# Attention on one core: seven single PSUM banks in a ring, exponentials by half units, maxima cut in two parts on GpSimd

## The chip, the core and the metric

The kernel runs on one core of a Trainium2 chip. The metric is device time in microseconds; three runs of the kernel before had a median of 1662.29 us (1660.99 to 1663.57). TensorE is called PE, VectorE DVE, ScalarE ACT, GpSimd POOL and SyncE SP, as in the profile.

## The reference

A two-layer block over 8 sequences of 512 tokens with 256 features: cross attention with 16 heads of 16 dimensions, a mixture of experts, a second cross attention, and a linear layer with simulated fp8. Only the two attentions matter here:

```python
qh = _split_heads(q @ q_map, R); kh = _split_heads(k @ k_map, R); vh = _split_heads(k @ v_map, R)
scores = jnp.einsum('brqd,brkd->brqk', qh, kh) * scale
weights = jax.nn.softmax(scores, axis=-1)
out = jnp.einsum('brqk,brkd->brqd', weights, vh)
```

## The kernel before

`attention(S, l)` runs twice, for l = 0 and l = 1. A *group* is one sequence and four heads; there are 32 groups (NG), n = 0 to 31, and each has 8 *units* (U), numbered i. The softmax subtracts a maximum for each query, and both the maximum and the exponential need a product of q and k, so the product is made twice:

- `max_unit` (L340) makes the products of two heads for 128 queries, two matmuls of 512 columns in a pair of PSUM banks. DVE's `take_maxima` (L346) reduces the pair to 2 numbers per query. The maxima run AHEAD = 14 units in front of the scores, so that of PE's 256 score units the first 242 (PAIRED) are each followed by a maximum unit.
- When the 8 maxima units of a group are reduced, `turn_maxima` on DVE cuts the maxima into a rounded part (a cast, L1137) and a remainder (a subtraction, L1139), and transposes both (L1143). SP moves them with four DMAs (`move_maxima`, L361) into rows of q of the group to come, where the score product subtracts them. PE's first score unit of that group waits for it (`mrow`).
- `score_unit` (L1062) makes the scores less maxima, two matmuls into another pair of banks; ACT takes the exponential of the whole pair (L1120, 128x1024) into SBUF.
- `values` (L1074) multiplies exponentials by values: for each unit half of a 128-key tile of an earlier unit, four matmuls (eight in the trace, two passes each), accumulating in `pout`. After a group's last one ACT copies `pout` to SBUF (L1111) and SP stores it (L996) and loads it back in another layout.
- POOL issues the ten DMAs that load q and k of the group four ahead (`load`, L415), once the scores of a group are all made and its buffers are free, and in layer 0 adds a bias to X once in four groups (L1043).

Each engine runs its own queue in the written order, with semaphores between them. PE's order for a unit is score, maximum, values. The eight PSUM banks are three pairs (`ring`) and two single banks (`pout`), and pairs go round over the uses maximum, score, maximum, score. So score unit s waits until maxima unit s-1 (counted from the 14 ahead) is reduced, and the maximum unit behind it waits until the exponential of score unit s-1 is taken:

```python
if s: e.wait_ge(reduced, s)
score_unit(n, i)
if s + 1 < PAIRED:
    if s: e.wait_ge(exped, s)
    max_unit(AHEAD + s + 1)
```

Of the kernel before, what the change touches and what calls it, by code (L numbers as in the profile page):

```python
# [14 lines left out]
P = 128  # L15
# [269 lines left out]
BLOCK = 32  # L285

# [49 lines left out]
def max_products(e, bank, q, k, i):  # L336
    t, p = i // 2, i % 2
    for hh in range(2):
        at = slice(HALF * hh, HALF * (hh + 1))
        mm = e.matmul(bank[:, hh, :], q[at, p, t * P:(t + 1) * P], k[at, p, :], start=True, stop=True)  # L340
    return mm


def take_maxima(e, nmax, bank, i):
    t, p = i // 2, i % 2
    return e.tensor_reduce(nmax[:, :].rearrange("p (x y t) -> p x y t", x=2, y=2)[:, :, p, t], bank[:, :, :],  # L346
                           AX.X, ALU.max, negate=True)

# [15 lines left out]
class Ahead:  # L364
# [7 lines left out]
    def make(self, e, m):  # L372
# [5 lines left out]
        max_products(e, self.banks[m % 2], self.inputs.q[n], self.inputs.k[n], m % UNITS).then_inc(self.made, 1)  # L378
# [555 lines left out]
def attention(S, l):  # L934
# [6 lines left out]
    with ctx:  # L941
# [8 lines left out]
        ring = [ps(f"ring{j}", [P, 2, SEQ]) for j in range(3)]  # L950
        pout = [ps(f"pout{j}", [P, SEQ]) for j in range(2)]
# [14 lines left out]
        def max_bank(m):  # L966
            return ring[(AHEAD + 2 * (m - AHEAD)) % 3]

        def score_bank(s):
            return ring[(AHEAD + 1 + 2 * s if s < PAIRED else AHEAD + PAIRED + s) % 3]  # L970

        def spread_bank(b, kd):
            return score_bank(NG * U - 3 + b)[:, kd, :]
# [10 lines left out]
        with nc.Block() as block:  # L984
# [40 lines left out]
            def _(e):  # L1025
# [3 lines left out]

                for j in range(EARLY_GROUPS, G):  # L1030
# [18 lines left out]
            def _(e):  # L1049
                def max_unit(m):  # L1050
# [3 lines left out]
                    max_products(e, max_bank(m), q[n % G], k[n % G], i).then_inc(maxed, 1)  # L1054

                def score_unit(n, i):
# [3 lines left out]
                    for hh in range(2):  # L1060
                        at = slice(HALF * hh, HALF * (hh + 1))
                        mm = e.matmul(score_bank(n * U + i)[:, hh, :], k[j][at, p, t * P:(t + 1) * P], q[j][at, p, :],  # L1062
# [3 lines left out]
                def values(n, t, half):  # L1066
                    b, g = n // G, n % G
                    if t == 0 and half == 0:
                        if n >= 2:
                            e.wait_ge(taken, n - 1)  # L1070
                    e.wait_ge(exped, n * U + 2 * t + 2)
                    at = slice(half * D, (half + 1) * D)
                    for h in range(HG):
                        mm = e.matmul(pout[n % 2][32 * h:32 * h + VW, at], v[:, b * TPB + t, g * HG + h, :], pexp[t][:, h, at],  # L1074
# [3 lines left out]
                e.wait_ge(clear, 2)  # L1078
                max_unit(AHEAD)
                for n in range(NG):  # L1080
                    for i in range(U):
                        s = n * U + i
                        if s < PAIRED:
                            if s:
                                e.wait_ge(reduced, s)
                        elif s == PAIRED + 1:
# [1321 lines left out]
```

## Time and profile before

| | |
|---|---|
| median of three runs | 1662.29 us |
| span of the profiled execution | 1670.2 us |
| attention l = 0 in the span, about | 120 to 457 us |
| attention l = 1 in the span, about | 1227 to 1563 us |
| DVE reduces of maxima in the two stages | 484, mean 1220 ns |
| ACT exponentials | 512, mean 1026 ns |
| ACT copies of outputs | 64, about 0.59 us |

The profiled execution is one execution, taken by the hardware profiler; its span runs from the first to the last instruction. Start times count from the span's start. In the timeline view a row holds like instructions of one engine merged, with start, duration and count, and in brackets the idle time before and what ended it. A score unit is a row L1062 on PE with x2, a maximum unit a row L340 with x2, values a row L1074 with x8. PEld is the load of the weights. Starts of the same engine's instructions are closer than their durations, since they are pipelined.

### The profile page before, as it was taken

The page shows a single profiled execution, that of the slowest core. Times are in us where ns is not written, and L with a number is a line of the kernel's source. Part 1 is how long each engine was busy: PE and PEld are TensorE (multiplying, and loading weights), DVE is VectorE, ACT ScalarE, POOL GpSimd, SP SyncE. Part 2 cuts the span into 40 slices and gives each one's busy share as a digit, 9 for nine tenths or more (in the row PEclk, how much of TensorE's full clock was granted, in tenths as well). Part 3 has the DMA queues.
Part 4 walks back from the last instruction along what each step waited for, and adds up shares of the span by engine and source line. Part 5 has one row for each costly group of instructions (what it writes and reads, how often), then busy time and mean ns, then how long its engine had stood idle before and what let it go on. Part 6 is the DMA issues. An engine that isn't in the chain of part 4 may idle for free. (4 is left out here: it accounts for less than half of the span.)

```text
span 1670.2 us, 28397 instructions
## 1 busy us (share of the span) xinstructions
PE 1513.5 (91%) x10910; PEld 979.2 (59%) x10910; DVE 1293.5 (77%) x2074; ACT 977.5 (59%) x1238; POOL 637.3 (38%) x957
## 2 busy tenths in 40 slices
PE   7989999999996289999999999779979999999846
PEld 6863333333385279999999999745523333333434
DVE  6789999999665856657665564379889999999787
ACT  5547888888833134444444444336548888888544
POOL 4314555555122135344342332255324444443120
PEclk9989999999996589999999999979979999999986
DMA  8974565555263022222223221168745555554103
GB/s 277 326 204 94 122 122 123 122 123 123 68 259 101 27 64 87 82 77 78 84 82 93 70 79 36 44 213 286 219 93 123 123 123 122 123 123 103 34 0 101
DMA packets 118742, 198.58 MB, mean 119 GB/s; under 512 B 29568, under 2 KB 63680, under 8 KB 117584
## 3 DMA queue, kind: packets, MB, share of 16 engines
q1 hardware_dynamic: 83840, 111.22, 21.9%
q0 software_dynamic: 33360, 83.94, 20.1%
q8 instruction: 87, 1.43, 0.4%
q10 hardware_dynamic: 1408, 1.61, 0.3%
q14 instruction: 47, 0.39, 0.1%
HBM read 117.77 MB, written 77.87 MB: 117 GB/s over the span
## 5 line engine op out<-in xcount | busy, mean ns | idle before, releaser
L1120 ACT ACTIVATE i_room<-a_ring 128x1024 f32<-128x1024 f32 x512 | 522.5, 1026 | 130.8 <-PE a_ring L1062 130.7
L346 DVE TENSOR_REDUCE logit<-a_ring 128x2 f32<-128x1024 f32 x484 | 576.9, 1220 | 26.7 <-PE a_ring L340 26.4
L1074 PE MATMUL a_pout<-i_room,values 128*17 128x256 f32 x4096 | 321.7, 387 | 0.7 <-ACT i_room L1120 0.7
L1755 ACT ACTIVATE e_full<-e_pH,b1T 128x320 f32<-128x320 f32 x256 | 135.0, 527 | 247.0 <-PE e_pH L1696 236.3
L1704 PE MATMUL e_pY<-fc_w,e_hid_hi 128*128 128x512 f32 x640 | 237.1, 407 | 0.6 <-DVE e_hid_lo L1808 0.6
L1062 PE MATMUL a_ring<-i_qk 64*128 64x512 f32 x768 | 194.9, 504 | 2.6 <-DVE logit L346 1.9
L1705 PE MATMUL e_pY<-fc_w,e_hid_lo 128*128 128x256 f32 x640 | 179.8, 281 | 0.0
L1062 PEld LDWEIGHTS a_ring<-i_qk 64*128 64x128 f32 x768 | 72.8, 186 | 169.7 <-DVE logit L346 103.1
L340 PE MATMUL a_ring<-i_qk 64*128 64x512 f32 x712 | 165.5, 461 | 6.0 <-DVE a_pout L1169 5.2
L1816 POOL DMA_INDIRECT w<-normed,slot_get x80 | 84.4, 1055 | 225.7 <-PE fc_turned L1681 199.6
L1808 DVE TENSOR_TENSOR e_hid_lo<-e_full,e_hid_hi 128x640 fp32r<-128x640 f32 x128 | 119.5, 934 | 55.7 <-ACT e_hid_hi L1764 55.7
L1696 PE MATMUL e_pH<-e_rowsT_hi,fc_w1T_hi 128*128 128x320 f32 x512 | 159.5, 312 | 0.0
L1696 PE MATMUL e_pH<-e_rowsT_lo,fc_w1T_hi 128*128 128x320 f32 x512 | 159.0, 311 | 0.0
L1696 PE MATMUL e_pH<-e_rowsT_hi,fc_w1T_lo 128*128 128x320 f32 x512 | 158.4, 309 | 0.0
L1074 PEld LDWEIGHTS a_pout<-i_room,values 128*17 128x17 f32 x4096 | 68.3, 95 | 129.7 <-issue 126.7
L1704 PEld LDWEIGHTS e_pY<-fc_w,e_hid_hi 128*128 128x128 f32 x640 | 120.3, 188 | 24.3 <-DVE e_hid_lo L1808 0.9
L1705 PEld LDWEIGHTS e_pY<-fc_w,e_hid_lo 128*128 128x128 f32 x640 | 121.3, 189 | 0.0
L1833 POOL DMA_INDIRECT ytok<-e_y,slot_put x80 | 82.7, 1034 | 93.0 <-DVE e_y L1788 78.3
L415 POOL DMA_DIRECT2D i_qk<-key_centre x42 | 24.1, 573 | 212.2 <-PE a_ring L1062 212.2
L1764 ACT ACTIVATE e_hid_hi<-e_full 128x640 fp32r<-128x640 f32 x128 | 94.6, 739 | 11.8 <-ACT e_full L1755 0.4
L1696 PEld LDWEIGHTS e_pH<-e_rowsT_hi,fc_w1T_hi 128*128 128x128 f32 x512 | 96.7, 189 | 5.6
L340 PEld LDWEIGHTS a_ring<-i_qk 64*128 64x128 f32 x712 | 67.9, 187 | 53.2 <-ACT i_room L1120 30.6
(334 smaller groups left out, 2530.2 us busy)
## 6 DMA issues: line engine op xcount, KB each, us to landing
ks<-i_room SPq DMA_DIRECT2D x64, 256.0 KB, 4.1
outs<-a_osb SPq DMA_DIRECT2D x64, 256.0 KB, 2.8
qs<-i_room SPq DMA_DIRECT2D x60, 256.0 KB, 4.7
fc_raw<-in_L_ffn_fc_w SPq DMA_DIRECT2D x15, 1024.0 KB, 5.4
i_qk<-ks POOLq DMA_DIRECT2D x84, 128.0 KB, 3.5
i_qk<-qs POOLq DMA_DIRECT2D x84, 128.0 KB, 3.6
BIG<-outs SPq DMA_DIRECT2D x64, 128.0 KB
ytok<-r_zeros SPq DMA_DIRECT2D x8, 1024.0 KB, 9.6
```

Of the source, the lines that this page charges most:

```text
L340: mm = e.matmul(bank[:, hh, :], q[at, p, t * P:(t + 1) * P], k[at, p, :], start=True, stop=True)
L346: return e.tensor_reduce(nmax[:, :].rearrange("p (x y t) -> p x y t", x=2, y=2)[:, :, p, t], bank[:, :, :], AX.X, ALU.max, negate=True)
L1062: mm = e.matmul(score_bank(n * U + i)[:, hh, :], k[j][at, p, t * P:(t + 1) * P], q[j][at, p, :], start=True, stop=True)
L1074: mm = e.matmul(pout[n % 2][32 * h:32 * h + VW, at], v[:, b * TPB + t, g * HG + h, :], pexp[t][:, h, at], start=(t == 0 and half == 0), st ...
L1120: e.activation(pexp[t][:, 2 * p:2 * p + 2, :], score_bank(n * U + i)[:, :, :], ACT.Exp).then_inc(exped, 1)
L1696: mm = e.matmul(pH[h][:, 0:WIDE], w1T[x][pl][:, k, f * P:(f + 1) * P], rowsT[j][pr][:, k, h * WIDE:(h + 1) * WIDE], start=(k == 0 and n_pa ...
L1704: e.matmul(pY[t][:, :, :], hid[s % 3][HI][:, token], w2[x][:, f, :, :], start=(f == 0), stop=False)
L1705: mm = e.matmul(pY[t][:, HI, :], hid[s % 3][LO][:, token], w2[x][:, f, HI, :], start=False, stop=(f == KF - 1))
L1755: e.activation(full[s % 2][:, h * WIDE:(h + 1) * WIDE], pH[h][:, 0:WIDE], ACT.Silu, bias=S.b1T[:, n * KF + f:n * KF + f + 1]).then_inc(act, 1)
L1764: e.activation(hid[s % 3][HI][:, :], full[s % 2][:, :], ACT.Copy).then_inc(hi, 1)
L1808: e.tensor_tensor(hid[s % 3][LO][:, :], full[s % 2][:, :], hid[s % 3][HI][:, :], ALU.subtract).then_inc(lo, 1)
L1816: e.indirect_dma_start(rows[:, t, :], None, S.normed[:, :], bass.IndirectOffsetOnAxis(ap=S.slot_get[:, c:c + 1], axis=0)).then_inc(ldr[0 i ...
```

## The change

- **PSUM.** The ring is one tensor of seven single banks, `pout` has one bank. A use takes two neighbouring banks modulo 7. Since 7 is odd, one maxima unit in seven falls on the last and the first bank; DVE reduces it in two instructions (`take_maxima_apart`).
- **ACT.** The exponential of a unit is two instructions of 128x512, each with its own signal. A maximum unit waits only for the first half of the unit before. Score units wait for the exponentials of two units before, too.
- **Values.** With one `pout`, the values that hang over from the group before are made in units 0 (one) and 1 (two) of a group, none in unit 2; ACT copies `pout` after unit 1 and not after unit 3.
- **Maxima.** POOL makes the two parts (`cut_maxima`). In its queue they stand behind the ten load DMAs. DVE transposes two units later than before.

```diff
+BANKS = 7
+VALUE_LAG = 3
+TURN_LAG = 2
+LATE_VALUES = (UNITS - 3,), (UNITS - 2, UNITS - 1)
...
+def take_maxima_apart(e, nmax, banks, i):
+    t, p = i // 2, i % 2
+    for hh in range(2):
+        last = e.tensor_reduce(nmax[:, :].rearrange("p (x y t) -> p x y t", x=2, y=2)[:, hh, p, t:t + 1], banks[hh],
+                               AX.X, ALU.max, negate=True)
+    return last
...
-        ring = [ps(f"ring{j}", [P, 2, SEQ]) for j in range(3)]
-        pout = [ps(f"pout{j}", [P, SEQ]) for j in range(2)]
+        ring = ps("ring", [P, BANKS, SEQ])
+        pout = ps("pout", [P, SEQ])
...
+                def cut_maxima(n):
+                    halves, whole = max_halves(nparts[n % 2]), max_whole(nmax[n % 2])
+                    if n >= 3:
+                        e.wait_ge(nturned, n - 2)
+                    e.wait_ge(reduced, (n + 1) * U - AHEAD)
+                    e.tensor_copy(halves[:, :, 0, :], whole).then_inc(cut, 1)
+                    e.wait_ge(cut, 2 * n - 1)
+                    e.tensor_tensor(halves[:, :, 1, :], whole, halves[:, :, 0, :], ALU.subtract).then_inc(cut, 1)
...
                 for n in range(NG):
-                    if n + G < NG:
-                        load(n + G)
+                    if 0 < n <= NG - G:
+                        load(n - 1 + G)
+                    if n + 1 < NG:
+                        cut_maxima(n + 1)
...
-                        if n >= 2:
-                            e.wait_ge(taken, n - 1)
-                    e.wait_ge(exped, n * U + 2 * t + 2)
+                    if t == 0 and half == 0 and n:
+                        e.wait_ge(taken, n)
+                    e.wait_ge(exped, 2 * (n * U + 2 * t + 2))
...
                         if s < PAIRED:
                             if s:
                                 e.wait_ge(reduced, s)
+                            if s >= 2:
+                                e.wait_ge(exped, 2 * s - 2)
...
                         if s + 1 < PAIRED:
                             if s:
-                                e.wait_ge(exped, s)
+                                e.wait_ge(exped, 2 * s - 1)
                             max_unit(AHEAD + s + 1)
-                        if i >= 3:
-                            values(n, (i - 3) // 2, (i - 3) % 2)
-                        elif n:
-                            values(n - 1, (i + U - 3) // 2, (i + U - 3) % 2)
+                        if i >= VALUE_LAG:
+                            values(n, (i - VALUE_LAG) // 2, (i - VALUE_LAG) % 2)
+                        elif n and i < VALUE_LAG - 1:
+                            for v_unit in LATE_VALUES[i]:
+                                values(n - 1, v_unit // 2, v_unit % 2)
...
-                        e.activation(pexp[t][:, 2 * p:2 * p + 2, :], score_bank(n * U + i)[:, :, :], ACT.Exp).then_inc(exped, 1)
-                        if i == 3 and n:
+                        for hh in range(2):
+                            e.activation(pexp[t][:, 2 * p + hh, :], score_bank(n * U + i, hh), ACT.Exp).then_inc(exped, 1)
+                        if i == 1 and n:
                             take_outputs(n - 1)
...
                 for m in range(AHEAD, NG * U):
                     reduce(m)
-                    if m % U == U - 1:
-                        turn_maxima(m // U)
+                    if m % U == TURN_LAG - 1 and m >= 2 * U:
+                        turn_maxima(m // U - 1)
+                turn_maxima(NG - 1)
```

On DVE, at the start of attention l = 0, before: eight reduces, then the cast, the subtraction and the transposition of a group's maxima.

```order
L346 TENSOR_REDUCE logit<-a_ring 128x2 x8
L1137 CAST logit<-logit 128x2x8
L1139 TENSOR_TENSOR logit<-logit 128x2x8
L1143 STREAM_TRANSPOSE logit<-logit 128x32
L346 TENSOR_REDUCE logit<-a_ring 128x2 x8
```

The same place now; L357 is a maxima unit reduced in two halves.

```order
L350 TENSOR_REDUCE logit<-a_ring 128x2 x6
L1175 STREAM_TRANSPOSE logit<-logit 128x32
L357 TENSOR_REDUCE logit<-a_ring 128x1 x2
L350 TENSOR_REDUCE logit<-a_ring 128x2 x6
L357 TENSOR_REDUCE logit<-a_ring 128x1 x2
L1175 STREAM_TRANSPOSE logit<-logit 128x32
```

The cast and the subtraction are gone from DVE, and 34 of its 242 reduces of an attention have become two.

On POOL, before, a group's work is ten load DMAs and nothing else (in layer 0 sometimes the bias):

```order
L415 DMA i_qk<-key_centre 8x2x512
L415 DMA i_qk<-query_centre 8x2x512
L415 DMA i_qk<-ks 32x2x512
L415 DMA i_qk<-qs 32x2x512
L415 DMA i_qk<-ks 16x2x512
```

Now, the end of one group's loads and the start of the next's:

```order
L427 DMA i_qk<-ks 16x2x512
L427 DMA i_qk<-qs 16x2x512
L1051 CAST logit<-logit 128x2x8 [waits a0_reduced,a0_nturned]
L1053 TENSOR_TENSOR logit<-logit 128x2x8 [waits a0_cut]
L427 DMA i_qk<-key_centre 8x2x512 [waits a0_scored]
L427 DMA i_qk<-query_centre 8x2x512
```

The two parts of the maxima stand behind all ten DMAs of a load that is released two units before the maxima are complete.

On PE, in the second unit of a group, now (before, each unit has one values part, L1074 x4, and the score unit waits only for `reduced`):

```order
L1089 MATMUL a_ring<-i_qk 128x512 [waits a0_exped,a0_reduced]
L1089 MATMUL a_ring<-i_qk 128x512
L344 MATMUL a_ring<-i_qk 128x512 [waits a0_ld0,a0_exped]
L344 MATMUL a_ring<-i_qk 128x512
L1100 MATMUL a_pout<-i_room,values 17x256 [waits a0_exped]
L1100 MATMUL a_pout<-i_room,values 17x256 x3
L1100 MATMUL a_pout<-i_room,values 17x256 [waits a0_exped]
L1100 MATMUL a_pout<-i_room,values 17x256 x3
L1089 MATMUL a_ring<-i_qk 128x512 [waits a0_exped,a0_reduced]
```

One values part has moved from the third unit into the second.

## Rows read from the trace of the kernel before

**Rows 1.** Busy time by engine in one stretch (us), granted clock, DMA share, GB/s

```profile
300.00:400.00 100.00, 99.86 (x918) 38.40 (x920) 95.03 (x107) 81.27 (x86) 55.90 (x100) 1.00 0.50 121
```

**Rows 2.** Timeline of all engines, 300 to 312 us: PE and ACT

```profile
301.89 0.50 PE L1062 MATMUL a_ring<-i_qk 64*128 64x512 f32 x2
302.22 0.41 PE L340 MATMUL a_ring<-i_qk 64*128 64x512 f32 x2
302.43 1.02 ACT L1120 ACTIVATE i_room<-a_ring 128x1024 f32<-128x1024 f32 x1 [0.35 <-PE a_ring L1062]
302.56 0.63 PE L1074 MATMUL a_pout<-i_room,values 128*17 128x256 f32 x8
303.11 0.51 PE L1062 MATMUL a_ring<-i_qk 64*128 64x512 f32 x2
303.50 0.50 PE L340 MATMUL a_ring<-a_k,a_q 64*128 64x512 f32 x2
304.49 0.50 PE L1062 MATMUL a_ring<-i_qk 64*128 64x512 f32 x2
```

**Rows 3.** Timeline of the same stretch: the turning of the maxima and its release

```profile
303.93 0.18 DVE L1137 CAST logit<-logit 128x16 fp32r<-128x16 f32 x1
304.42 0.21 DVE L1143 STREAM_TRANSPOSE logit<-logit 128x32 f32<-128x32 f32 x1
304.56 1.19 DVE L346 TENSOR_REDUCE logit<-a_ring 128x2 f32<-128x1024 f32 x1
...
305.80 0.19 PEld L1062 LDWEIGHTS a_ring<-i_qk 64*128 64x128 f32 x2 [0.52 <-DVE logit L346]
```

**Rows 4.** Timeline of the same stretch: POOL's ten loads

```profile
300.50 0.51 PE L1062 MATMUL a_ring<-i_qk 64*128 64x512 f32 x2
...
301.31 0.57 POOL L415 DMA_DIRECT2D i_qk<-key_centre  x1 [5.30 <-PE a_ring L1062]
...
306.05 0.50 POOL L415 DMA_DIRECT2D i_qk<-qs  x1
...
311.83 0.57 POOL L415 DMA_DIRECT2D i_qk<-key_centre  x1 [5.28 <-PE a_ring L1062]
```

**Rows 5.** Timeline of ACT in the same stretch: output copy, next exponential

```profile
307.27 0.59 ACT L1111 ACTIVATE a_osb<-a_pout 128x512 f32<-128x512 f32 x1
307.75 1.03 ACT L1120 ACTIVATE i_room<-a_ring 128x1024 f32<-128x1024 f32 x1
```

**Rows 6.** Single lines: durations ns min/median/max, first and last start

```profile
L263 POOL TENSOR_TENSOR r_product<-r_mv,r_rstd x8: 198/198/198, 471.8 to 515.4; 128x4 f32<-128x4 f32 x8
L1043 POOL TENSOR_TENSOR X<-X,bo_b x8: 2380/2390/2398, 148.6 to 422.4; 128x1024 f32<-128x1024 f32 x8
```

**Rows 7.** Timeline outside attention: small POOL operations, alone and beside DVE

```profile
75.49 0.21 POOL L241 TENSOR_SCALAR p_var<-p_mv 128x4 f32<-128x4 f32 x1 [6.29 <-DVE p_mv L236]
...
1184.12 1.19 DVE L447 TENSOR_TENSOR i_room<-c_full_k,i_room 128x1024 fp32r<-128x1024 f32 x1
...
1184.29 1.11 POOL L241 TENSOR_SCALAR c_var<-c_mv 128x4 f32<-128x4 f32 x1 [3.72 <-DVE c_mv L236]
1185.48 1.03 POOL L244 TENSOR_TENSOR c_rstd<-c_var,half 128x4 f32<-128x4 f32 x1
```

**Rows 8.** Timeline, 1097 to 1099 us: a DVE instruction that waits for POOL

```profile
1097.71 1.12 POOL L244 TENSOR_TENSOR c_rstd<-c_var,half 128x4 f32<-128x4 f32 x1
1098.94 0.48 DVE L1945 SCALAR_TENSOR_TENSOR X<-BIG,c_rstd,X 128x256 f32<-128x256 f32 x1 [0.22 <-POOL c_rstd L244]
```

**Rows 9.** Timeline of POOL at the start of attention: first two loads

```profile
133.30 0.68 POOL L415 DMA_DIRECT2D i_qk<-key_centre  x1 [10.55 <-PE a_ring L1062]
...
143.35 0.57 POOL L415 DMA_DIRECT2D i_qk<-key_centre  x1 [4.69 <-PE a_ring L1062]
```

**Rows 10.** SP in the stretch of Rows 2, and the landing of output stores

```profile
304.66 2.63 SPq L361 DMA_DIRECT2D i_qk<-logit  x4
DMA to landing us min/median/max: 2.0/2.8/4.3
```

More of the change, by code:

```diff
@@ L333, in load_half, with max_products @@
             load_group(self.S, self.l, e, n, self.q[n], self.k[n], self.ld[n], range(half * (LOADS // 2), (half + 1) * (LOADS // 2)))
-def max_products(e, bank, q, k, i):
+def max_products(e, banks, q, k, i):
     t, p = i // 2, i % 2
@@ L339, in max_products, with take_maxima @@
         at = slice(HALF * hh, HALF * (hh + 1))
-        mm = e.matmul(bank[:, hh, :], q[at, p, t * P:(t + 1) * P], k[at, p, :], start=True, stop=True)
+        mm = e.matmul(banks[hh], q[at, p, t * P:(t + 1) * P], k[at, p, :], start=True, stop=True)
     return mm
-def take_maxima(e, nmax, bank, i):
+def take_maxima(e, nmax, pair, i):
     t, p = i // 2, i % 2
-    return e.tensor_reduce(nmax[:, :].rearrange("p (x y t) -> p x y t", x=2, y=2)[:, :, p, t], bank[:, :, :],
+    return e.tensor_reduce(nmax[:, :].rearrange("p (x y t) -> p x y t", x=2, y=2)[:, :, p, t], pair[:, :, :],
                            AX.X, ALU.max, negate=True)
+def take_maxima_apart(e, nmax, banks, i):
[4 more added lines that the diff above has]
+    return last
 def max_halves(nparts):
@@ L377, in make @@
             e.wait_ge(self.taken, m - 1)
-        max_products(e, self.banks[m % 2], self.inputs.q[n], self.inputs.k[n], m % UNITS).then_inc(self.made, 1)
+        max_products(e, [self.banks[m % 2][:, hh, :] for hh in range(2)], self.inputs.q[n], self.inputs.k[n], m % UNITS).then_inc(self.made, 1)
     def take(self, e, m):
@@ L964, in attention, with max_first, max_banks, score_bank @@
         oput = [sem(f"oput{j}") for j in range(2)]
[L966 to L970, printed above, removed]
+        def max_first(m):
+            return 4 * (m - AHEAD) % BANKS
+        def max_banks(m):
+            return [ring[:, (max_first(m) + hh) % BANKS, :] for hh in range(2)]
+        def score_bank(s, hh):
+            use = 2 * s + 1 if s < PAIRED else PAIRED + s
+            return ring[:, (2 * use + hh) % BANKS, :]
         def spread_bank(b, kd):
-            return score_bank(NG * U - 3 + b)[:, kd, :]
+            return ring[:, b * KD + kd, :]
         def moved(n):
@@ L1053, in max_unit @@
                         loaded(e, n)
-                    max_products(e, max_bank(m), q[n % G], k[n % G], i).then_inc(maxed, 1)
+                    max_products(e, max_banks(m), q[n % G], k[n % G], i).then_inc(maxed, 1)
                 def score_unit(n, i):
@@ L1110, in take_outputs @@
                         e.wait_ge(oput[n % 2], 16 * (n // 2))
-                    e.activation(osb[n % 2][:, :], pout[n % 2][:, :], ACT.Copy).then_inc(taken, 1)
+                    e.activation(osb[n % 2][:, :], pout[:, :], ACT.Copy).then_inc(taken, 1)
                 inputs.wait_stored(e)
@@ L1131, in reduce @@
                     e.wait_ge(maxed, m + 1 - AHEAD)
-                    take_maxima(e, nmax[n % 2], max_bank(m), m % U).then_inc(reduced, 1)
-                def turn_maxima(n):
-                    halves, whole = max_halves(nparts[n % 2]), max_whole(nmax[n % 2])
-                    e.wait_ge(reduced, (n + 1) * U - AHEAD)
-                    e.tensor_copy(halves[:, :, 0, :], whole).then_inc(cut, 1)
-                    e.wait_ge(cut, 2 * n - 1)
-                    e.tensor_tensor(halves[:, :, 1, :], whole, halves[:, :, 0, :], ALU.subtract).then_inc(cut, 1)
+                    first = max_first(m)
+                    if first + 1 < BANKS:
+                        take_maxima(e, nmax[n % 2], ring[:, first:first + 2, :], m % U).then_inc(reduced, 1)
+                    else:
+                        take_maxima_apart(e, nmax[n % 2], max_banks(m), m % U).then_inc(reduced, 1)
+                def turn_maxima(n):
                     if n >= 3:
```

19 lines of the change are left out of this document (10 added, 9 removed).

## The prediction

> **What bounds the kernel now.** I read the busy times by stretch first, then the timeline of one group of attention, then single lines. In attention PE is busy 99.86 of 100 us at full granted clock, DVE 95, ACT 81 [rows 1]; three engines so close together say that a loop between them may bind rather than one engine. The repeat is exact: POOL's load of one group starts at 301.31 and the next at 311.83, a period of 10.52 us for 8 units, 1.315 us a unit [rows 4].
>
> The timeline shows two kinds of unit. From one score unit to the next PE takes 303.11 - 301.89 = 1.22 us, called 1.23 below, when nothing holds it; the next takes 304.49 - 303.11 = 1.38 [rows 2]. What holds it is the exponential: score at 301.89, exponential from 302.43 for 1.02, and the maximum unit at 303.50 needs that pair of banks; then 0.99 to the score unit at 304.49. This loop over two units costs 2.60 us, 1.30 a unit [rows 2]. DVE adds a little: its turn runs from the cast at 303.93 to the next reduce at 304.56, and the score unit behind it starts at 305.80, released by DVE [rows 3]. So now: PE's own 8 x 1.23 = 9.84 us, and 0.68 of waits, nearly all for ACT and the turn.
>
> **The change, part by part.**
>
> *ACT in halves.* An instruction of 128x512 lasts 0.59, and the next starts 307.75 - 307.27 = 0.48 behind it [rows 5]. The chain above becomes 0.54 + 0.59 + 0.05 + 0.99 = 2.17 us for two units, under PE's 2.46: the wait is gone, alone worth up to about 0.6 us a group. ACT itself needs 17 x 0.48 = 8.2 us a group and is hidden behind PE; were that cover gone it would add nothing until 9.84.
>
> *DVE without cast and subtraction.* From 303.93 to 304.42 DVE is rid of 0.49 us a group [rows 3]. One maxima unit in seven is two reduces of 512 columns. No reduce of 512 columns from PSUM is shown; on ACT two halves last 2 x 0.59 against 1.02 for the whole, 0.16 more [rows 2, 5]. I bound the split by nothing and 0.2, hidden except where DVE has the deciding reduce (some 4 groups of 28, 0.03 a group on average), and take 0.
>
> *Values doubled in unit 1.* A values part takes 303.11 - 302.56 = 0.55 [rows 2]. Unit 1 lasts 1.23 + 0.55, unit 2 is as much shorter. PE's sum is unchanged, but the maxima unit behind the third score comes later, which DVE reaches late in turn. ACT's copy meets that gap.
>
> *The cuts on POOL.* Here the stall goes. Let L be the start of a group's load. The ten DMAs run from 301.31 to 306.05 + 0.50 = 306.55, 5.24 us [rows 4]. The cuts stand behind them, though the maxima are complete at L + 2.6 (303.93 against 301.31) [rows 3, 4]. DVE asks for them two units later: the last score of the group before is at L - 0.81 (300.50 against 301.31) [rows 4], so scores 0 and 1 are at L + 0.42 and L + 1.65, score 2 is 1.78 later at L + 3.43; its maximum product comes 0.33 later and is reducible about 0.45 behind its start (estimate, it lasts 0.41 and DVE must wake), and the reduce needs 1.22, so DVE is at the transposition at L + 5.4. POOL is not ready: cast 0.21, by the small one-input operation at 75.49 [rows 7]; a gap to the dependent one of 0.08, as at 1185.40 to 1185.48 [rows 7]; subtraction 0.22, from 0.198 for 4 columns [rows 6] plus 12 columns at 2.1 ns (2390 ns for 1024); 0.11 until DVE starts, as from 1098.83 to 1098.94 [rows 8]; 0.05 for the gap behind the last DMA and a second wait (estimate). Together 0.67, ready at L + 5.91. DVE stalls 0.5 us in each group, and this becomes a loop of its own:
>
> - transposition to next reduce 0.14, reduce 1.19, score 0.05: 305.80 - 304.42 = 1.38 [rows 3]
> - two more units to the last score of the group, at PE's pace: 2.46 [rows 2]
> - that score to the next load: 0.81 [rows 4]
> - ten DMAs: 5.24 [rows 4]
> - cuts and wakes: 0.67
>
> That is 10.56 us, against 10.52 now. The gains in ACT, PE and DVE all fall inside the stall; the loop doesn't contain them.
>
> May POOL's small operations be much dearer? At 1184.29 L241 took 1.11 us, at 75.49 the same operation took 0.21. The long one overlaps a DVE operation with two SBUF inputs that ends at 1185.31, and it ends just behind it, at 1185.40 [rows 7]. In attention DVE reduces from PSUM, and the bias addition directly behind loads is constant at 2380 to 2398 ns [rows 6]. So I take the low value, with 1.11 as the upper bound.
>
> The Trainium skill (GPSIMD Engine Reference, Key points) says that GpSimd shares its SBUF interfaces with VectorE and contends with instructions in a 2-port mode or with two SBUF inputs; the two rows agree, and by it the low price holds here, since neither reduce nor transposition is of that kind.
>
> The same page (Engine selection) speaks against the change: two-input elementwise work belongs on VectorE, GpSimd being about twice as slow; by that the subtraction would be an estimated 0.35 rather than 0.22, and the total some 7 us more, which the 198 ns row does not bear out.
>
> *The move, two units later.* The four DMAs start 0.24 behind the transposition and take 2.63 to issue, the last starting at about + 2.25 [rows 3, 10]. The first score of the next group is at + 1.38 + 3 x 1.23 = + 5.07. So the last DMA has 2.8 us to land, and DVE's 0.5 of slack takes in 0.4 more. Small DMAs show no landing here; output stores of 256 KB land in 2.0 to 4.3, median 2.8 [rows 10]. A 4 KB one should be near the low end: I cost it at nothing. SP's stores and reloads of outputs, behind it in its queue, come two units later; ACT needs that buffer only a group later.
>
> *Sum.* Each attention has 28 loads, 27 periods. The first was short, 143.35 - 133.30 = 10.05 [rows 9], and becomes 10.56: + 0.5. The other 26 gain 0.04 each: + 1.0. Behind the last load no cut is late: about 13 units with maxima remain, at 1.23 instead of 1.315, - 1.1, with + 0.3 for a doubled values part and + 0.2 for the later start, so - 0.6. The 14 units without maxima stay. Together + 0.9, twice + 1.8 us. The profiled execution spans 1670.2, so I expect a span of about 1672; it is 7.9 us over the median, and the same difference on the median of 1662.3 gives 1664.
>
> **The rivals.**
>
> 1. *The cuts are dearer than priced* (slower). Place: POOL behind the ten DMAs. Each 0.1 us costs 54 x 0.1 = 5.4 us, as nothing absorbs it. For it: small POOL operations of 0.5 to 1.1 exist [rows 7], and none of 16 columns is shown. Against: the 2380 to 2398 ns. A cast of 0.5 gives + 16, 1680; of 1.1, + 48, 1712. It decides from + 0.03 us a group.
> 2. *The moved maxima land late* (slower). Above 3.2 us from issue each 0.1 costs 5.4 us: at 3.8, some + 30, 1694. For it: median 2.8 of the stores, and loads in flight. Against: 4 KB, and 2.0 as the least.
> 3. *POOL is a little quicker* (faster): cuts and wakes in 0.55 instead of 0.67 make the period 10.44 and the total - 6.5 + 1.8, about 1657.5.
> 4. *The cuts come in time* (faster), the change doing what halves and ring allow: then the period is 9.84 plus the 0.3 that the doubled values cost, 10.15, giving 54 x 0.37 = 20 us and the ends' 2: 1640. Against: POOL would have to be done by L + 5.4, and its DMAs alone need 5.24.
> 5. *Nothing changes in the period because PE bounds anyway*: excluded by the 1.22 and 1.38 in turn [rows 2].
>
> **How the numbers follow.** Forecast 0.55, rival 1 0.20, rival 2 0.08, rival 3 0.12, rival 4 0.05. Within 0.2% is 3.3 us, about what a measurement of this kernel can tell from no change. Of the forecast's 0.55 about 0.07 falls above 1665.6 (cuts of 0.70 and more) and 0.01 below; so faster 0.18, same 0.47, slower 0.35. The range reaches from rival 3 to the milder half of rival 1: 1656 to 1681. That leaves out rivals 2 and 4 and the dear half of rival 1, 0.2 together. The forecast's own range is 1659 to 1668.
>
> **What would show it.** Right: load starts on POOL 10.5 to 10.6 apart; the cast starting where the tenth DMA ends; the transposition waiting for POOL about 0.5 us in each group; no wait of the maximum units for ACT; score intervals of 1.23 in units 5 to 7, and about 1.8 and 0.7 around unit 2. Wrong: loads 10.15 apart with no wait on POOL (rival 4); a cast of 0.5 or more (rival 1); first score units waiting for the maxima's DMA (rival 2).

## The result

The changed kernel takes 1673.08 us (1671.99 to 1674.41, four runs) against 1662.57 for the kernel before on the same chip (1660.99 to 1663.57): a ratio of 1.0069, 95% interval 1.0054 to 1.0083. It is slower by 0.7%, 10.5 us. The forecast was 1664, the likeliest outcome "within 0.2%"; the time lies in the range of 1656 to 1681, on the slower side. One execution each of two kernels below (3413.7 and 1717.46 us), far above the others of its kernel, is left out of the numbers given.

The profiled execution of the kernel before was 7.9 us above its median, and the excess lies outside attention (the rest of its span is 1002.4 us, in the other thirteen profiles 991.3 to 999.3), so I compare the two attention stages. From the first score unit to the last they took 333.9 and 333.9 us before, 337.5 and 338.8 now: + 8.4 us. The other 2 us of the 10.5 between the medians are not placed by these two profiles. From the first load of a group to the 28th, 27 periods, it was 283.8 and 283.9, and is 289.5 and 290.9.

Busy time by engine of the kernel after, in the stretch of [rows 1], and in three short stretches that are spoken of below:

```profile
core 0: us, PE busy (x) PEld busy (x) DVE busy (x) ACT busy (x) POOL busy (x), PEclk, DMA share, GB/s
300.00:400.00 100.00, 91.87 (x894) 34.01 (x888) 88.51 (x94) 83.67 (x158) 60.29 (x116) 0.98 0.58 120
370.00:372.00 2.00, 1.13 (x4) 0.50 (x4) 1.94 (x2) 0.30 (x1) 0.00 (x0) 0.68 0.03 4
372.00:374.00 2.00, 2.00 (x14) 0.65 (x12) 1.23 (x1) 0.95 (x3) 0.00 (x0) 0.50 0.25 88
374.00:376.00 2.00, 2.00 (x24) 0.64 (x22) 1.74 (x2) 1.68 (x4) 0.49 (x1) 0.97 0.33 99
```

In the first 100 us PE is busy 91.87 us where it was 99.86, DVE 88.51 where it was 95.03. No engine is full any more: the loop that binds has idle time in every one of them.

The timeline of one group, kernel after; POOL, then DVE and SP, then PE. These rows answer to [rows 2 to 4]:

```profile
319.95 0.57 POOL L427 DMA_DIRECT2D i_qk<-key_centre  x1 [4.97 <-PE a_ring L1089]
...
324.69 0.50 POOL L427 DMA_DIRECT2D i_qk<-qs  x1
325.19 0.21 POOL L1051 CAST logit<-logit 128x16 fp32r<-128x16 f32 x1
325.48 0.21 POOL L1053 TENSOR_TENSOR logit<-logit 128x16 fp32r<-128x16 f32 x1
330.41 0.57 POOL L427 DMA_DIRECT2D a_k<-key_centre  x1 [4.71 <-PE a_ring L1089]
...
324.02 1.23 DVE L350 TENSOR_REDUCE logit<-a_ring 128x2 f32<-128x1024 f32 x1 [0.35 <-PE a_ring L344]
325.80 0.21 DVE L1175 STREAM_TRANSPOSE logit<-logit 128x32 f32<-128x32 f32 x1 [0.56 <-POOL logit L1053]
325.94 3.44 DVE L350 TENSOR_REDUCE logit<-a_ring 128x2 f32<-128x1024 f32 x3
329.30 1.28 DVE L357 TENSOR_REDUCE logit<-a_ring 128x1 f32<-128x512 f32 x2
...
326.04 2.64 SPq L373 DMA_DIRECT2D i_qk<-logit  x4
...
324.52 0.50 PE L344 MATMUL a_ring<-i_qk 64*128 64x512 f32 x2 [0.30 <-ACT i_room L1153]
325.51 0.50 PE L1089 MATMUL a_ring<-a_q,a_k 64*128 64x512 f32 x2
327.17 0.50 PE L1089 MATMUL a_ring<-a_q,a_k 64*128 64x512 f32 x2 [0.38 <-DVE logit L350]
328.39 0.50 PE L1089 MATMUL a_ring<-a_q,a_k 64*128 64x512 f32 x2
329.61 0.50 PE L1089 MATMUL a_ring<-a_q,a_k 64*128 64x512 f32 x2
```

Read as the loop of the prediction, with L = 319.95: ten DMAs to 325.19 (L + 5.24), the cast directly behind them, the transposition at 325.80 (L + 5.85) after DVE has waited 0.56 us for POOL, a score unit 1.37 later at 327.17, two more in 2.44, and the next load 0.80 behind that, at 330.41. The period is 10.46 us. The page's list of waits has it in sum, beside the second row that matters, first score units that wait for the moved maxima:

```profile
DVE logit L1175 <- POOL logit L1053: 34.0, 50, 2.3
PE a_ring L1089 <- DMA i_qk<-logit: 4.7, 7, 1.2
```

Most of the 54 periods measure 10.45 to 10.60. Nine do not: 12.98, 13.63, 13.63 and 13.71, always the 13th and the 23rd of an attention; 10.71 right behind the first of them; and 10.97, 10.71, 11.23 and 11.31. POOL's timeline in the first of the long ones, then what DVE and PE do behind it:

```profile
257.81 0.53 POOL L427 DMA_DIRECT2D i_qk<-qs  x1
260.11 0.50 POOL L427 DMA_DIRECT2D i_qk<-ks  x1 [1.77 <-issue]
260.61 0.50 POOL L427 DMA_DIRECT2D i_qk<-qs  x1
261.11 0.21 POOL L1051 CAST logit<-logit 128x16 fp32r<-128x16 f32 x1
...
261.72 0.21 DVE L1175 STREAM_TRANSPOSE logit<-logit 128x32 f32<-128x32 f32 x1 [2.33 <-POOL logit L1053]
...
263.10 0.51 PE L1089 MATMUL a_ring<-i_qk 64*128 64x512 f32 x2 [2.16 <-DVE logit L350]
265.98 0.79 PE L1089 MATMUL a_ring<-i_qk 64*128 64x512 f32 x2
```

POOL stands still for 1.77 us between the eighth and the ninth DMA of a load, for nothing that the profile shows. PE then idles 2.16 us, and soon behind it the two matmuls of the score unit at 265.98 last 0.79 instead of 0.50 us. The stretches above show the second such place: behind the pause the granted clock is 0.68 from 370 to 372 and 0.50 (1.2 of 2.4 GHz) from 372 to 374, and is back at 0.97 from 374 to 376. It falls to 0.50 behind each of the four pauses (0.50 or 0.51 in 265:268, 371:374, 1371:1374 and 1480:1483).

The pause is no work of the change. The kernel before has it too, in the same two loads of each attention:

```profile
262.92 0.53 POOL L415 DMA_DIRECT2D i_qk<-qs  x1
265.22 0.51 POOL L415 DMA_DIRECT2D i_qk<-ks  x1 [1.76 <-issue]
265.72 0.50 POOL L415 DMA_DIRECT2D i_qk<-qs  x1
269.73 0.57 POOL L415 DMA_DIRECT2D i_qk<-key_centre  x1 [3.51 <-PE a_ring L1062]
```

There POOL waits for PE 3.51 us behind it, so it cost nothing.

### The profile page after: what moved, and what is told of

Read it like the earlier page. It is cut to its first block and busy times, and to the rows that moved or that the text cites. A ratio compares the mean times of both kernels' runs of the same rounds, so it can differ in the third digit from the quotient of the medians.

```text
span 1672.0 us, 29457 instructions
## 1 busy us (share of the span) xinstructions
PE 1470.5 (88%) x10910; PEld 954.5 (57%) x10910; DVE 1265.5 (76%) x2016; ACT 1008.9 (60%) x1750; POOL 662.8 (40%) x1081
## 3 DMA queue, kind: packets, MB, share of 16 engines
q8 instruction: 88, 1.44, 0.4%
## 5 line engine op out<-in xcount | busy, mean ns | idle before, releaser
L1153 ACT ACTIVATE i_room<-a_ring 128x512 f32<-128x512 f32 x1024 | 547.3, 609 | 99.3 <-PE a_ring L1089 62.0
L350 DVE TENSOR_REDUCE logit<-a_ring 128x2 f32<-128x1024 f32 x416 | 491.3, 1218 | 32.7 <-PE a_ring L344 29.8
L1100 PE MATMUL a_pout<-i_room,values 128*17 128x256 f32 x4096 | 311.6, 388 | 3.3 <-ACT i_room L1153 1.8
L1089 PE MATMUL a_ring<-i_qk 64*128 64x512 f32 x768 | 190.7, 494 | 23.7 <-DVE logit L350 15.5
L1089 PEld LDWEIGHTS a_ring<-i_qk 64*128 64x128 f32 x768 | 73.2, 187 | 180.3 <-DVE logit L350 127.7
L1100 PEld LDWEIGHTS a_pout<-i_room,values 128*17 128x17 f32 x4096 | 74.8, 96 | 172.8 <-ACT i_room L1153 115.0
L344 PE MATMUL a_ring<-i_qk 64*128 64x512 f32 x712 | 149.6, 416 | 16.8 <-ACT i_room L1153 12.7
L1728 PEld LDWEIGHTS e_pH<-e_rowsT_lo,fc_w1T_hi 128*128 128x128 f32 x512 | 96.9, 189 | 0.0
```

Of the source, the lines that this page charges most:

```text
L344: mm = e.matmul(banks[hh], q[at, p, t * P:(t + 1) * P], k[at, p, :], start=True, stop=True)
L1089: mm = e.matmul(score_bank(n * U + i, hh), k[j][at, p, t * P:(t + 1) * P], q[j][at, p, :], start=True, stop=True)
L1100: mm = e.matmul(pout[32 * h:32 * h + VW, at], v[:, b * TPB + t, g * HG + h, :], pexp[t][:, h, at], start=(t == 0 and half == 0), stop=(t = ...
L1153: e.activation(pexp[t][:, 2 * p + hh, :], score_bank(n * U + i, hh), ACT.Exp).then_inc(exped, 1)
L1728: mm = e.matmul(pH[h][:, 0:WIDE], w1T[x][pl][:, k, f * P:(f + 1) * P], rowsT[j][pr][:, k, h * WIDE:(h + 1) * WIDE], start=(k == 0 and n_pa ...
```

## The experiments

All times are medians, and the ratios are against the kernel before on the same chip (1663.12 us for the first four kernels, 1663.51 for the next four, 1660.61 for the last four). "Period" is the distance of load starts in steady groups.

### The cuts back on DVE, still two units late

```diff
 # GpSimd: cut_maxima and its calls are gone; VectorE:
                 def turn_maxima(n):
+                    e.wait_ge(reduced, (n + 1) * U - AHEAD)
+                    e.tensor_copy(halves[:, :, 0, :], whole).then_inc(cut, 1)
+                    e.wait_ge(cut, 2 * n - 1)
+                    e.tensor_tensor(halves[:, :, 1, :], whole, halves[:, :, 0, :], ALU.subtract).then_inc(cut, 1)
```

> The changed kernel with cast and subtraction back on DVE, directly ahead of the transposition, which stays two units late. Theory A (GpSimd's queue sets the period: load, cuts, transposition, three reduces, last score, next load, 5.85 + 1.37 + 2.44 + 0.80 = 10.46 us, plus some 15 us in all of pauses inside the loads that now reach the path): DVE arrives at L + 5.3 and cuts for 0.5, so the transposition starts at about L + 5.8 again, the period stays near 10.4, but pauses of GpSimd no longer reach the path: 1655 us. Theory B (the loss sits in the ring of seven, the halved exponentials or the doubled values, and GpSimd is only where the wait shows): about 1670 to 1673.

Measured: 1683.0 us, ratio 1.0112 (1.0090 to 1.0133), against about 1655 expected. Both theories missed. Layer 1 did what was expected: period 10.30, 283.2 us for the 27 periods. Layer 0 took 301.9, with periods of 12.6 to 14.8 in six of the seven places within them where POOL adds the bias, which only layer 0 has. DVE and POOL at such a place:

```profile
178.43 1.23 DVE L350 TENSOR_REDUCE logit<-a_ring 128x2 f32<-128x1024 f32 x1 [0.36 <-PE a_ring L344]
179.57 2.46 DVE L1163 CAST logit<-logit 128x16 fp32r<-128x16 f32 x1
182.06 0.17 DVE L1165 TENSOR_TENSOR logit<-logit 128x16 fp32r<-128x16 f32 x1
...
179.62 2.37 POOL L1059 TENSOR_TENSOR X<-X,bo_b 128x1024 f32<-128x1024 f32 x1
```

A cast whose median is 165 ns lasts 2.46 us, until POOL's addition of two SBUF tensors is over. The same holds at seven of the eight additions, with casts of 1.99 to 2.99 us. The two periods of 12.60 ran at full clock (1.00 in 316:322 and 360:366); the four of 14.0 to 14.8 have a granted clock of 0.50 behind the wait (137:143, 185:188, 229:232 and 404:409), so part of the loss is the clock's. Both theories took the cuts on DVE as cheap; beside this addition they are not. A later kernel tests that by itself.

### The cuts amid the load

The same work on the same engines; POOL cuts between its fifth and sixth DMA. `load(n, part)` issues the first or the second five.

```diff
                 for n in range(NG):
                     if 0 < n <= NG - G:
-                        load(n - 1 + G)
+                        load(n - 1 + G, 0)
                     if n + 1 < NG:
                         cut_maxima(n + 1)
+                    if 0 < n <= NG - G:
+                        load(n - 1 + G, 1)
```

> The changed kernel with the cuts on GpSimd between the fifth and the sixth load DMA. Theory A: the cuts are done by about L + 3.3, long before DVE asks at L + 5.3, so neither the wait nor the pauses (which come behind the eighth DMA) reach the path; what is left is PE's own sequence of score intervals without the long one, 10.0 to 10.1 us a group: 1673 - 15 - 54 x 0.4 = 1636 us. Theory B: 1670 to 1673. If the later half load comes too late, first maximum units wait for it and the period is above 10.3.

Measured: 1639.0 us, ratio 0.9854 (0.9837 to 0.9870), period 10.01 to 10.02, 273.2 and 272.8 us for the 27 periods. POOL and DVE in one group:

```profile
311.11 0.51 POOL L427 DMA_DIRECT2D i_qk<-ks  x1
311.61 0.21 POOL L1052 CAST logit<-logit 128x16 fp32r<-128x16 f32 x1
311.91 0.22 POOL L1054 TENSOR_TENSOR logit<-logit 128x16 fp32r<-128x16 f32 x1
312.07 0.52 POOL L427 DMA_DIRECT2D i_qk<-qs  x1
...
312.98 1.23 DVE L350 TENSOR_REDUCE logit<-a_ring 128x2 f32<-128x1024 f32 x1 [0.35 <-PE a_ring L344]
314.12 0.20 DVE L1178 STREAM_TRANSPOSE logit<-logit 128x32 f32<-128x32 f32 x1
```

The transposition follows a reduce with no wait. So the place of the cuts in POOL's queue, not the work, costs the changed kernel about 34 us, pauses included. Rival 4 gave 1640 for cuts in time.

### The cast twice

A dose: one more cast on POOL in each group.

```diff
                     e.wait_ge(reduced, (n + 1) * U - AHEAD)
+                    e.tensor_copy(halves[:, :, 0, :], whole).then_inc(twice, 1)
+                    e.wait_ge(twice, n)
                     e.tensor_copy(halves[:, :, 0, :], whole).then_inc(cut, 1)
```

> The changed kernel with GpSimd's cast made twice. Theory A: the loop has no slack, each group grows by the cast and its gap, 0.21 + 0.08 = 0.29 us, over 54 periods: + 16 us, 1689 us, and load starts 10.75 apart. Theory B (other engines set the pace): within 3 us of 1673.

Measured: 1682.3 us, ratio 1.0108 (1.0088 to 1.0128). The period is 10.74, expected 10.75: 0.28 for the dose, nothing absorbed. The total is only 9.3 us above the changed kernel where 16 were expected. The traces say where the rest is: the four long periods are 12.49 each here (10.74 + 1.75, the bare pause) and not 12.98 to 13.71, and the moves cost less (five first scores waited 2.7 us in sum). Over all 54 periods 8.1 us stand above the steady ones, against 15.6 in the changed kernel. PE idled 2.42 us behind a pause here, longer than in the changed kernel, and its clock stayed at 1.00, behind all four. So what a pause costs in clock differs from kernel to kernel, and I can't say from these traces what decides it.

### The kernel before with POOL's cuts alone

The diff is that of the change in `cut_maxima`, its place behind the loads, and the transposition two units later; pairs of banks, whole exponentials and the values stay as before.

> The kernel before with one part of the change alone: cuts on GpSimd behind the loads, transposition two units later; ring of three pairs, whole exponentials and two output banks stay. Theory A: the loop is 1.38 + 2 x 1.315 (PE held by the exponentials) + 0.80 + 5.24 + 0.61 = 10.66 us instead of 10.52, plus the pauses, some 11 us in all, plus 1: about 1681 us, slower than the whole change. Theory B: about 1660 to 1663, as the kernel before.

Measured: 1682.5 us, ratio 1.0113 (1.0097 to 1.0130), period 10.63 (expected 10.66). The half of the change that moves the cuts costs 19 us alone. The row that says so is DVE's wait:

```profile
307.53 0.21 DVE L1149 STREAM_TRANSPOSE logit<-logit 128x32 f32<-128x32 f32 x1 [0.65 <-POOL logit L1037]
```

Its four periods with a pause also separate the pause from the clock. PE idles 1.89 to 1.90 us behind each pause. Two of the periods are 12.40, the bare pause over 10.63, at a clock of 1.00; the other two are 13.72 and 14.37, with a clock of 0.53 in 375:378 and 0.50 in 1379:1385. The first two rows are the start of the work behind a pause that kept the clock and behind one that lost it, the third is the score unit behind the latter:

```profile
266.37 0.50 PE L1073 MATMUL a_ring<-i_qk 64*128 64x512 f32 x2 [1.89 <-DVE logit L346]
374.48 0.50 PE L1073 MATMUL a_ring<-a_q,a_k 64*128 64x512 f32 x2 [1.90 <-DVE logit L346]
376.13 0.79 PE L1073 MATMUL a_ring<-a_q,a_k 64*128 64x512 f32 x2
```

### The cuts on DVE as soon as the maxima are complete

```diff
                 for m in range(AHEAD, NG * U):
                     reduce(m)
-                    if m % U == TURN_LAG - 1 and m >= 2 * U:
-                        turn_maxima(m // U - 1)
-                turn_maxima(NG - 1)
+                    if m % U == U - 1:
+                        turn_maxima(m // U)
```

with the cast and subtraction in `turn_maxima`, as in the first experiment.

> Ring of seven, halved exponentials and late values kept; cast, subtraction and transposition on DVE as soon as the maxima are complete, as in the kernel before. Theory A with the collision seen in the first run of cuts on DVE (DVE's cast lasted 2.5 to 3.0 us where GpSimd's bias addition ran): here the cast comes at about L + 1.7 to 2.6, the addition at L + 5.3, so they don't meet; DVE has room for the 0.6 us in the gap of the doubled values, and the period is PE's 10.0: about 1639 us, as with the cuts amid the load. Theory B (cuts on DVE are what costs, wherever they stand): 1655 or more.

Measured: 1636.6 us, ratio 0.9844 (0.9819 to 0.9869), period 10.09. This is the ring of seven banks, the halves and the values of the change with the maxima handled as before. They are worth 27 us. DVE's turn stands well ahead of where POOL adds the bias.

### The transposition a unit later still

```diff
-TURN_LAG = 2
+TURN_LAG = 3
```

> The changed kernel with the transposition three units late instead of two. Theory A: DVE asks at L + 6.5, GpSimd is ready at L + 5.85, so the wait on GpSimd is gone and half of the pauses with it. Then the move of the maxima decides: the last DMA starts at L + 6.5 + 2.2 = L + 8.7, the first score unit of the next group wants it at about L + 10.4, so it has 1.7 us. If a small DMA lands in under 1.7 us: 10.0 and about 1642 us. If it lands in 2.0 to 2.5 us: 0.3 to 0.8 late each group, a loop of its own at 10.3 to 10.8: 1655 to 1680 us, with the first score unit of a group waiting for the DMA. Theory B: no change, 1673.

Measured: 1661.5 us, ratio 1.0000 (0.9980 to 1.0021, ten runs). With one unit more of slack POOL is in time but for six groups: many periods are 10.01. The 13th and 23rd of each attention, with the pause in them, are 11.01. Between them stand others up to 11.5, and PE's waits name the cause:

```profile
PE a_ring L1089 <- DMA i_qk<-logit: 15.3, 20, 1.4
```

20 first scores wait for the move, against seven in the changed kernel. The first score comes 1.8 to 3.3 us behind the start of the last of the four DMAs in these cases. This is rival 2, nearly alone: late moves take back what POOL's punctuality gives.

### The halves in the old ring

The kernel before, with exponentials of 128x512; each of the two maximum products waits for its half.

```diff
+                    for hh in range(2):
+                        if m > AHEAD + 1:
+                            e.wait_ge(exped, 2 * (m - AHEAD - 2) + 1 + hh)
+                        at = slice(HALF * hh, HALF * (hh + 1))
+                        mm = e.matmul(max_bank(m)[:, hh, :], q[n % G][at, p, t * P:(t + 1) * P], k[n % G][at, p, :], start=True, stop=True)
```

> The kernel before with one part of the change alone: each exponential in two halves, and each of the two maximum matmuls waits for its half; ring of three pairs, cuts on DVE. Theory: the second half ends 0.54 + 0.49 + 0.59 = 1.62 us behind the score against 1.56 for the whole, so the maximum unit waits as long as before and the period stays at 10.5: 1663 us within 3; the halves pay only with the seventh bank. If halves alone free PE: 10.0, 1635.

Measured: 1677.1 us, ratio 1.0093 (1.0067 to 1.0118), where no change was expected. Period 10.71. The maximum unit that was held now starts early and waits in its middle:

```profile
302.13 0.49 PE L1068 MATMUL a_ring<-i_qk 64*128 64x512 f32 x2
302.47 0.62 PE L1059 MATMUL a_ring<-a_k,a_q 64*128 64x512 f32 x2
303.01 0.63 PE L1080 MATMUL a_pout<-i_room,values 128*17 128x256 f32 x8
303.57 0.50 PE L1068 MATMUL a_ring<-i_qk 64*128 64x512 f32 x2
...
301.45 2.31 ACT L1125 ACTIVATE i_room<-a_ring 128x512 f32<-128x512 f32 x4 [0.35 <-PE a_ring L1068]
```

It lasts 0.62 where a free one takes 0.40, and the held unit is 303.57 - 302.13 = 1.44 us (1.38 before). Two halves take 1.08 us where the whole took 1.02, and the second bank of the pair is needed in the same unit. So halves alone are a loss. With the seventh bank, where the two neighbouring banks come free from different units, they are part of the 27 us gained above. No run has the seven banks with whole exponentials, so what each of the two gives there is not separated.

### The bias addition behind the turn

The first experiment, with POOL's addition held until DVE's turn of that group is over.

```diff
                     if l == 0 and n % G == 1:
+                        e.wait_ge(nturned, n + 1)
                         x = S.X[:, tiles(n // G), :]
```

> The first experiment (cuts on DVE, two units late) with one edit: GpSimd's bias addition in layer 0 waits for the transposition. Theory C (DVE's cast and GpSimd's two-input addition exclude each other, in layer 0 alone): the casts last 0.17 again, layer 0 becomes as fast as layer 1 of that run, where 28 loads took 283 us instead of 302: 1683 - 20 = 1663 us. If the stalls stay, something else of that kernel makes them: 1680 or more.

Measured: 1659.9 us, ratio 0.9983 (0.9967 to 0.9999, ten runs). Layer 0 takes 281.6 us for its 27 periods, after 301.9 in the first experiment, and layer 1 282.8 (283.2). The 20 us were the collision and what followed it, the clock included, since one wait takes them away: all of DVE's casts last 0.16 to 0.18 us here.

### The centre rows loaded by SP

Two of a load's ten DMAs go from POOL to SP, with a semaphore of their own.

```diff
+                    if 0 < n <= NG - G:
+                        m = n - 1 + G
+                        e.wait_ge(scored, (m - G + 1) * U)
+                        load_group(S, l, e, m, q[m % G], k[m % G], ld_first[m % G], range(2))
...
-                    load_group(S, l, e, n, q[n % G], k[n % G], ld[n % G], range(LOADS))
+                    load_group(S, l, e, n, q[n % G], k[n % G], ld[n % G], range(2, LOADS))
```

> The changed kernel with two of a load's ten DMAs (the key and query centres) issued by SP instead of GpSimd. Theory A: GpSimd's load takes 10 - 2 DMAs = 4.1 us, the cuts are done at about L + 4.7, before DVE asks at L + 5.3: no wait, 10.0 to 10.1 us a group, about 1640 us. The pauses: if they go by the number of GpSimd's DMAs (they stood behind the 128th and the 228th of 280 of each attention in every kernel so far, with other instructions between or not), then the first one now stands behind the last DMA of the 16th load, ahead of the cut, and costs about 1 us, and the second one does not come (224 DMAs); if they go by the program's position, they stay in the 13th and 23rd load. Theory B (GpSimd's load is not what decides): 1670.

Measured: 1638.2 us, ratio 0.9866 (0.9848 to 0.9884), period 10.01. POOL is done 1.13 us earlier, and that is enough. One period in each attention is long, 12.75 and 12.55; it is that behind the 16th load. POOL's timeline there:

```profile
281.02 0.50 POOL L427 DMA_DIRECT2D a_q<-qs  x1
281.52 0.21 POOL L1056 CAST logit<-logit 128x16 fp32r<-128x16 f32 x1
281.81 0.22 POOL L1058 TENSOR_TENSOR logit<-logit 128x16 fp32r<-128x16 f32 x1
290.15 0.55 POOL L427 DMA_DIRECT2D i_qk<-ks  x1 [8.13 <-PE a_ring L1094]
```

The DMA at 281.02 is POOL's 128th of this attention, as the one ahead of the pause was before. The next starts at 290.15, and its row puts the idle time down to PE. But SP's two DMAs of the same load wait for the same score unit, and they start at 287.43 and 287.76:

```profile
287.43 0.29 SPq L427 DMA_DIRECT2D i_qk<-key_centre  x1
```

In most loads POOL's first DMA starts 0.17 to 0.27 us behind SP's first; here it starts 2.72 behind it, and 2.72 in the second attention too. So POOL stood still with its wait already over, though it had done nothing for over 5 us before. With eight DMAs in a load the 128th ends the 16th load, and the pause comes three periods later than with ten. The second pause, after the 228th, is gone, since only 224 DMAs are issued. So the pause goes by the number of POOL's DMAs and not by time or group. What POOL does in it, no run shows.

### Values two units late, none doubled

The cuts amid the load, and in addition:

```diff
-VALUE_LAG = 3
+VALUE_LAG = 2
-LATE_VALUES = (UNITS - 3,), (UNITS - 2, UNITS - 1)
+LATE_VALUES = (UNITS - 2,), (UNITS - 1,)
```

> The kernel with the cuts amid the load, and no doubled values: values follow two units behind instead of three, so that the last two parts of a group fall into units 0 and 1 of the next. In the kernel with the cuts amid the load a group's score intervals are 1.22, 1.65, 0.57, 1.70, then four of 1.22, 10.02 in all. Theory: eight of 1.22 are 9.76, but the first values part must wait for ACT's copy of the output, about 0.25, so 10.0 and no gain, 1639 within 3. If ACT's copy is hidden: 9.8 and 1627. If the exponentials of the last two units are too late for it: 10.3 or more, 1654.

Measured: 1635.5 us, ratio 0.9851 (0.9831 to 0.9870), period 10.05. The doubled unit is gone, seven distances are 1.22 and one is 1.51; there the values wait for ACT's copy of `pout`:

```profile
309.18 0.63 PE L1103 MATMUL a_pout<-i_room,values 128*17 128x256 f32 x8 [0.21 <-ACT a_osb L1146]
```

Eight free units would be 9.76 us. The single bank of `pout` costs about 0.3 us a group over that, with values doubled (10.02) or without (10.05).

### The cuts amid the load, the transposition one unit earlier; and DVE's cuts again

```diff
-TURN_LAG = 2
+TURN_LAG = 1
```

> The kernel with the cuts amid the load, transposition one unit late instead of two. Nine of its 62 first score units waited for the moved maxima (landed 3.1 to 4.0 us behind the issue of the last DMA). Theory: with 1.2 us more none waits, the period stays 10.0, total 1 to 4 us less: 1636 us. If late moves are not what those long intervals are: unchanged 1639.

Measured: 1635.9 us, ratio 0.9853 (0.9836 to 0.9869); all periods 10.00 to 10.03 but two, no wait for the moves. Beside it, the kernel with DVE's cuts as soon as the maxima are complete was run again:

> The kernel with ring of seven, halved exponentials and cuts and transposition on DVE at once, again, beside the one with cuts on GpSimd: 1636.6 expected as before. It tells whether GpSimd's cuts are worth anything once they are in time: theory, within 3 us of the neighbour, since PE sets the pace in both.

Measured: 1637.6 us, ratio 0.9857 (0.9839 to 0.9874), period 10.09. Where POOL is in time its cuts are worth 0.07 us a group, and in the medians nothing that these runs can tell. No version found is faster than these two. With the ones of values two late and of the cuts amid the load, whose intervals overlap with theirs, they are 1.4 to 1.6% faster than the kernel before, and about 2.2% faster than the change.

## Why the prediction was wrong by 9 us

The mechanism was right in its place and its parts. It was the sum over the 54 periods that left something out.

- **Period.** Forecast 10.56, steady 10.46. The ten DMAs 5.24 (5.24), cuts and wakes 0.61 (0.67), transposition to score 1.37 (1.38), two units 2.44 (2.46), last score to load 0.80 (0.81). Cast and subtraction took 0.208 and 0.216 us as medians, constant (0.193 to 0.222): rival 1 is out. The forecast's 10.56 was 0.10 too long, which by itself took 5.4 us off the miss. By the period alone the change would have gained 0.06 us x 54 = 3.3 us, rival 3's result.
- **The step that failed: "ten DMAs: 5.24", taken for each load.** In two loads of each attention they take 7.01, with the pause in them. The kernel before hid it behind POOL's wait for PE, and its trace showed it (above). The change put POOL on the path. The four periods cost 53.95 - 4 x 10.46 = 12.1 us, and the one of 10.71 behind the first 0.3: 4 x 1.77 = 7.1 is the pause, 5.3 what followed it, with the clock at 0.50 behind each pause. That this is the clock's price is measured where the pause is the same and the clock is not: 12.40 against 13.72 and 14.37 in the kernel before with POOL's cuts, and 12.49 in all four places of the one with the cast twice. For the second place of the changed kernel that can be read off PE: three score units from 370.87 stand 2.13 and 1.70 apart instead of 1.22, 1.4 us, all of 13.63 - 10.46 - 1.77, and they lie in the two stretches of low clock. The prediction had no term for either.
- **The moves.** "I cost it at nothing" held in most groups. Four periods were longer by 2.4 us in sum, with first scores that waited up to 1.2 us for the moved maxima. Rival 2 was true in part: a stop now and then, not each group. The prediction had no landing of a small move; the semaphore updates in the traces have it. The last of the four moves ends 1.72 to 4.15 us behind its issue in the kernel before (median 3.6), where moves are issued amid a load, and 1.71 to 3.94 (median 1.8) in the changed one, where they come behind it.
- **DVE's split reduce.** Two reduces of 512 columns have the engine for 1.19 us (the next reduce behind the pair at 329.30 begins at 330.49). From the start of a whole one to the next reduce, where nothing is waited for, the median is 1.13. So the split costs 0.06, off the path, and the value taken, nothing, was fair.
- **The ends.** Behind the last loads - 0.6 each was forecast, and both together gained 1.1 us. Another 3.2 us were gained ahead of the first loads, which the prediction gave no term.
- **Sum.** The 54 periods of the kernel after are 580.4 us, 15.6 over 54 x 10.46 = 564.8: 12.4 behind the pauses, 2.4 for moves, 0.8 of small ones. Those of the kernel before are 567.7. That is + 12.7, and with the ends - 4.3 it is the + 8.4 of the two stages.
- **The range held by luck in part.** Its slower side stood for dearer cuts, and these were cheaper than priced; the pauses fell into the room left for them. The likeliest outcome, within 0.2%, did not come; slower had been given 0.35.
- **The signs.** Load starts 10.46 apart are just outside the 10.5 to 10.6 named; the cast behind the tenth DMA, DVE's wait (median 0.56) and intervals of 1.22 came as named, those around unit 2 were 1.65, 0.57 and 1.70. One sign failed: in each group one maximum unit waits 0.30 us for ACT (324.52 above), behind the doubled values. Inside the stall it costs nothing; where POOL is in time it is about the 0.26 us between 10.02 and 9.76.
- **What was hidden.** "The gains in ACT, PE and DVE all fall inside the stall" is confirmed: with POOL in time (three ways: cuts amid the load, fewer DMAs, cuts on DVE at once) the same ring and halves run at 10.0 to 10.1. Rival 4's 10.15 and 1640 were close; what spoke against it, POOL's ten DMAs, was a matter of their order only.
- **One step of the argument is wrong though its result held**: that the ring takes nothing in the loop. The kernel before with POOL's cuts alone has 10.63, 0.17 more than the change, since the two units behind the turn run at the old pace in it.

The Trainium skill (SBUF — State Buffer, SBUF: two separate sides) describes the pair of SBUF ports that VectorE and GpSimd share as a lock, held for a whole instruction by whichever started first. It holds this for an operation of VectorE that uses both ports or has two SBUF inputs. The trace of the first experiment agrees in that the cast stood 2.46 us, to the end of a 2.37 us addition on GpSimd. Who started first it does not confirm: in five of the seven meetings the cast's recorded start is 0.04 to 0.57 us ahead of the addition's, and no run here shows which ports the cast uses. The prediction looked only for the other direction, VectorE holding GpSimd.

## What to carry to other kernels

Before an engine that always had slack is put on the path, look through its whole queue for pauses that the slack hid, in every repeat and not in one period, and give each its price. When work goes to an in-order queue, ask at which instruction its inputs are ready and at which they are wanted: cuts placed between the fifth and sixth DMA gave 34 us that cuts behind the tenth had lost. And where one part of a change is worth 27 us and the other, which costs 19 alone, takes 37 from it, only running the parts alone shows it, since the one on the path hides the gain of the other.

## What the runs showed of the hardware

- GpSimd's queue pauses behind the 128th and the 228th DMA that it issues in an attention, in all thirteen profiles with ten DMAs a load: 1.75 to 1.77 us in ten of them, 2.08 to 2.09 in the three of kernels with the cuts amid the load. With eight DMAs a load it stands behind the 128th all the same, where the next DMA comes 2.72 us behind its neighbour on SP.
- Of VectorE and GpSimd, the cast of SBUF data on the one (0.165 us) and an addition of two SBUF tensors on the other (2.37 us) exclude each other: the cast then lasts up to 2.99 us. The meetings cost the first experiment 20 us, part of it by the clock.
- Moves of 4 KB from SBUF to SBUF, issued by SP, end 1.71 to 4.15 us behind their issue in the kernels before and after (the last of each four): at a median of 3.6 amid a load and of 1.8 behind it.
- Whether TensorE's granted clock falls behind an idle of 2 us is not settled by these runs: it fell to 0.50 behind 2.14 to 2.16 us in all four places of the changed kernel, behind 1.90 in two of four places of the kernel before with POOL's cuts, and behind 2.42 in none of four of the one with the cast twice.
